# Cutting the first sequence into 256, 256 and 512 tokens and the last into 512, 384 and 128, in a software pipeline that took 512 tokens at a time

## What is computed

```python
x = L0_attn_x                                   # 4 x 1024 x 256
x = _layernorm(x + _L0_attn_ref(x, ...))        # conv, gates, recurrence h = a*h + b, out_w, RMS norm
x = _layernorm(x + relu(x @ W1 + b1) @ W2 + b2)
x = _layernorm(x + _L1_attn_ref(x, ...))        # in_proj, conv, x_proj, 16 states, out_proj
x = _layernorm(x + relu(x @ w1 + b1) @ w2 + b2)

def step(h, inp):                               # the state-space block, for each token t
    dA_t, dBx_t, C_t = inp
    h = dA_t * h + dBx_t                        # 256 channels x 16 states
    y_t = jnp.einsum('bdn,bn->bd', h, C_t)
    return (h, y_t)
```

## Time and profile before

| | us |
|---|---|
| median of 3 runs (1019.75 to 1020.57) | 1020.5 |
| the profiled execution, its own time | 1020.38 |
| its span, first to last instruction | 1018.6 |
| busy in the span: PE / DVE / ACT / POOL | 788.0 / 800.8 / 604.5 / 556.9 |

### The profile page before, as it was taken

The page is one execution under the profiler, slowest core; times in us unless marked ns, Lnnn a source line. Parts: engine busy times, 40 slices in busy tenths (PEclk is TensorE's granted clock), DMA queues, the critical chain, the costliest instruction groups (busy, mean ns, idle before and its releaser), DMA issues. The chain is left out here.

```text
span 1018.6 us, 8402 instructions
## 1 busy us (share of the span) xinstructions
PE 788.0 (77%) x2536; PEld 484.5 (48%) x2536; DVE 800.8 (79%) x970; ACT 604.5 (59%) x983; POOL 556.9 (55%) x419
## 2 busy tenths in 40 slices
PE   1439639855998999899979997999799796469275
PEld 0216225523553755475537553755375545226134
DVE  0400331999899999999999999999999999999711
ACT  3432745575758685868586858685857473443131
POOL 3041162257845785589457855894576466545510
PEclk9659878977999999999999999999999898589588
DMA  9000000000000010001000100010000000000000
GB/s 319 10 21 21 0 21 11 11 0 21 1 0 1 1 62 1 0 1 63 0 2 1 62 1 0 1 42 0 1 1 21 1 1 1 21 0 1 21 1 21
DMA packets 9213, 19.41 MB, mean 19 GB/s; under 512 B 1360, under 2 KB 3920, under 8 KB 9168
## 3 DMA queue, kind: packets, MB, share of 16 engines
q1 hardware_dynamic: 9168, 18.88, 5.4%
HBM read 14.68 MB, written 4.19 MB: 19 GB/s over the span
## 5 line engine op out<-in xcount | busy, mean ns | idle before, releaser
L350 POOL TENSOR_TENSOR y<-y,hC 128x1024 f32<-128x1024 f32 x112 | 271.9, 2428 | 120.0 <-DVE hC L915 116.9
L1102 PE MATMUL pC<-w,hT 128*128 128x256 f32 x1024 | 229.6, 379 | 2.3 <-ACT hT L546 2.3
L608 ACT ACTIVATE dA<-dt,A_neg 128x512 f32<-128x512 f32 x256 | 173.1, 715 | 89.2 <-DVE hs L904 88.9
L1102 PEld LDWEIGHTS pC<-w,hT 128*128 128x128 f32 x1024 | 194.0, 190 | 34.1 <-issue 4.7
L1223 PE MATMUL pS<-stack,sel 97*128 97x512 f32 x256 | 146.1, 604 | 73.7 <-DVE hs L904 73.6
L904 DVE TENSOR_TENSOR_SCAN hs<-dA,carry,pS 128x512 f32<-128x512 f32 x128 | 163.0, 1273 | 3.9 <-issue 0.4
L904 DVE TENSOR_TENSOR_SCAN hs<-dA,pS 128x512 f32<-128x512 f32 x128 | 155.3, 1214 | 9.0 <-DVE pS L889 5.4
L889 DVE TENSOR_TENSOR pS<-u,pS 128x1024 f32<-128x1024 f32 x128 | 154.9, 1210 | 2.1 <-PE pS L1223 1.8
L915 DVE TENSOR_TENSOR hC<-hs,pS 128x1024 f32<-128x1024 f32 x128 | 153.1, 1196 | 1.5 <-PE pS L1223 1.3
L1095 PE MATMUL pA<-tg,w 128*128 128x512 f32 x256 | 123.0, 623 | 16.4 <-ACT xi L554 14.5
L546 ACT ACTIVATE hT<-pA,ffb_sb 128x512 f32<-128x512 f32 x128 | 86.3, 682 | 82.6 <-PE pA L1095 82.6
(11 more groups left out here) (104 smaller groups left out, 1006.5 us busy)
## 6 DMA issues: line engine op xcount, KB each, us to landing
xt<-xT SPq DMA_DIRECT2D x8, 515.0 KB, 4.9
xtok<-x SPq DMA_DIRECT2D x8, 512.0 KB, 4.6
out<-x3b SPq DMA_DIRECT2D x8, 512.0 KB, 2.8
w<-w1a SPq DMA_DIRECT2D x1, 1024.0 KB, 9.1
w<-w2a SPq DMA_DIRECT2D x1, 1024.0 KB, 10.8
w<-w1b SPq DMA_DIRECT2D x1, 1024.0 KB, 8.3
w<-w2b SPq DMA_DIRECT2D x1, 1024.0 KB, 9.9
gate_w<-gateT SPq DMA_DIRECT2D x1, 512.0 KB, 7.0
```

Of the source, the lines that this page charges most:

```text
L350: nc.gpsimd.tensor_tensor(y[:, :, 0:ch.T], so_far, hC[:, n % CRING, :, 0:ch.T], ALU.add).then_inc(S["y_sum"], 1)
L608: nc.scalar.activation(dA[:, k % ARING, 0:ch.T], dt[:, h, 0:ch.T], ACT.Exp, scale=A_neg[:, h, n:n + 1]).then_inc(S["dA_ready"], 1)
L1102: mm = nc.tensor.matmul(dst[:, b * D:b * D + D], src(k, t0), w[:, k, :], start=k == 0, stop=k == nk - 1)
```

## The change

One line differs. It changes chunk lengths and with them the number of chunks, from 8 to 10, and of steps, from 12 to 14.

```diff
-SPLITS = ((512, 512), (512, 512), (512, 512), (512, 512))
+SPLITS = ((256, 256, 512), (512, 512), (512, 512), (512, 384, 128))
```

## The result

The changed kernel takes 1030.6 us (median of 4 runs, 1030.29 to 1030.95) where the kernel before, run beside it, takes 1020.5 (4 runs). The ratio is 1.0099, with a 95% interval of 1.0082 to 1.0117: 1% slower, 10.1 us. The prediction had slower as the likeliest side and 1024.3 us, 3.8 us more than before: the direction came, at well over twice the size.

The account below looks back on a forecast made before the run. VectorE was taken to bound full periods, one dependent chain the fill and drain. Front +4.4, middle -3.2 and -3.2, end +5.9 gave +3.9: span 1022.5, time 1024.3 us with 1.8 around it; range 1004 to 1038.

Parts of the forecast that it names:

- each step also holds the whole gate chain of a 512-token chunk, in order: Periods of chunks 0 and 1: the neighbour's chain sets their length, 78 and 90 us, against 57 and 65 DVE needs.
- Case A: Whole kernel: the ends gain, the short periods next to them hand it back; 1016 to 1032 us, centre 1024.3, chance 0.44.
- Rival B: Short periods of chunks 0 and 1 follow DVE and PE, near 66 and 76 us; centre 1011, chance 0.34.
- D: Whole kernel: fixed cost and gain cancel, DVE idle time falling by just 21 us; 1020.5 to 1025 us, chance 0.05.
- Rival C: Short states beside long PE blocks: DVE-PE round trip loses 0.4 us more in each of 32, +12, 1036 us; chance 0.17.
- If DVE waits on `pS` make more than 15 us in all, C is: Sign for the round-trip rival: DVE's waits for PE's spreads, summed, exceed 15 us.
- not on PE's spreads: Sign for the first two periods: DVE idle 20 to 25 us each, longest waits on ACT and POOL gate-chain pieces.
- 57 to `up`: Chunk 1's period: gate chain takes 57 us up to `up`, after a start of 12.5, within a 90 us period.
- 91.3: Chunk 7's period in us, with a prep chunk of 384 (-1.6) and a gate chunk of 128 (+4); before, 87.99.
- 17, 29 and four states of 1.6 to 2: Chunk 9's period: `up` at 17 us, 29 for `up`, `down`, spreads and waits, then four last states; put at 51.
- the first products of each burst run at 1.2 GHz: PE in the fill's step 0: granted clock 0.76; a burst after idle time loses about 2.7 us that half length doesn't halve.
- VectorE sets the pace: Full periods, such as chunk 2's: DVE busy 98.65 of 102.30 us is the bound; PE at 93.77 is close but not.

## Why the prediction was right

What it said would be seen, against the trace:

| | predicted | measured |
|---|---|---|
| first `u` | 109 | 110.3 |
| period of chunk 0 | 78 | 78.8 |
| of chunk 1 | 90 | 92.5 |
| of chunk 2 | 99 | 98.0 |
| of chunks 3 to 5 | 102 | 102.0, 102.0, 102.4 |
| of chunk 6 | 99 | 99.2 |
| of chunk 7 | 91.3 | 94.2 |
| of chunk 8 | 74.5 | 73.3 |
| of chunk 9 | 51 | 52.1 |
| drain | 24.5 | 23.8 |
| span | 1022.5 | 1028.5 |

The mechanism was right in its step "each step also holds the whole gate chain of a 512-token chunk, in order": the runs with the later norm, with quarters and with the cut in the middle show it for the front, and the one with halved products for the end. Case A came in, near its upper end. Rival B (the short periods follow DVE and PE) is out: they were 78.8 and 92.5, not 66 and 76. D had the work nearly right (DVE +25.0 busy, of which I had 21; 2.2 of the rest are the long `u` below), and the idle time wrong, as B had.

Rival C needs more care, because its sign came. "If DVE waits on `pS` make more than 15 us in all, C is": they make 26.3 + 9.3 = 35.6 us in the changed kernel, against 3.1 before. The rows for the whole span, after and then before:

```profile
DVE pS L889 <- PE pS L1223: 26.3, 15, 3.4
DVE hC L915 <- PE pS L1223: 9.3, 7, 2.7
```

```profile
DVE pS L889 <- PE pS L1223: 1.8, 2, 1.4
DVE hC L915 <- PE pS L1223: 1.3, 2, 0.9
```

8.4 us of them are in chunk 0's period, 11.1 in chunk 1's and 14.1 in chunk 9's, and so the sign "not on PE's spreads" for the first two periods didn't come either. What didn't come is C's price. It was 12 us on top of A, and the three periods that hold these waits are together 4.4 us above A's figures (223.4 against 219). So the sign was badly chosen: the spreads stand in PE's stream among the products of the long neighbour, and a chain that runs in order makes DVE wait for them too. A and C share this part. At the end it is the PE blocks ahead of the spreads (halving them moved the end by 5.7 us); in chunk 0's period 3 us on POOL, with no work on PE or DVE, moved it by 3.3, which C doesn't give.

The size was off by 6 us, in three terms (2.5, 2.9 and 1.3; the other marks take some 0.7 back):

- "57 to `up`" in chunk 1's period measured 60.2, and `up` up to the spread behind it 16.0 where I had 15.5, with its first eight products in 5.70 us; the start (12.2) and the rest (4.1) were 0.3 and 0.9 shorter than I had them. Together +2.5.
- "91.3" for chunk 7 measured 94.2. 2.2 us of this are its opening `u`, which lasted 3.42 us instead of 1.22:

```profile
785.13 5.65 POOL L350 TENSOR_TENSOR y<-y,hC 128x1024 f32<-128x1024 f32 x2
785.16 3.42 DVE L877 SCALAR_TENSOR_TENSOR u<-dt,v 128x1024 f32<-128x1024 f32 x1
```

A POOL sum began 0.03 us ahead of it; the two sums took 5.65 us, where two in a row take 4.86 elsewhere in this trace. The long `u` recurred with 3.42 us in the runs with the later norm and with halved products, was 1.37 in the one with doubled outputs and 1.55 in the run with only the last cut. In that last one POOL's sums began 0.43 us behind `u` and took 5.86 us. So it hangs on how the two meet; what they share there was not tried.
- The first `u` came 1.3 us later than 109, all of it in step 1 (47.3 us where I had 46); which link of its chain was longer I can't say.

Two sums of the prediction don't come out as they are written, and their slips cancel. The parts of chunk 9's period (17, 29 and four states of 1.6 to 2) give 52.4 to 54 and not 51; it measured 52.1. What is taken off the drain (20.5, 4.3, 9 and 2) leaves 22.7 and not 24.5; it measured 23.8. And "the first products of each burst run at 1.2 GHz" holds in step 0 for the output product and `up`, with a granted clock of 0.50 in the first 2.3 and 3.7 us, but not for the gate products, which stand at 1.00 although 16 of them took 9.37 us, against 7.03 in step 1.

The reading of the prediction that the runs refute didn't enter the sum: "VectorE sets the pace" in a full period. It does (18.2 us more of busy DVE time in chunk 4's period made it 17.7 longer), but the chain through POOL sets the same pace: 3.95 us more there made chunk 3's period 4.4 longer, so it had no slack to speak of.

## What to carry to other kernels

In this software pipeline, written in one fixed order, a step was at least as long as the longest role in it, so shortening one chunk gained only where its neighbours in the pipeline were short too. Look at each step's roles before you cut: at the front 256, 384, 384 won 7 us where 256, 256, 512, with the same number of chunks, lost 6. It is no rule for both ends, since 384, 384, 256 at the end lost 7. And a tightly ordered loop may sit on two bounds at once: an engine that is 97% busy is no proof that a delay elsewhere is free. Last, choose a sign that only one of the rivals gives: a wait that both give decides nothing.

## What the hardware showed that I had not expected

The state of PE's clock moved times by about 2 us a place in both directions: eight products of 512 columns took 3.60 to 3.70 us at a granted clock of 1.00, and 5.29 to 5.70 at 0.64 to 0.68. A delay of 3 to 4 us in the chain gave 2 back in this way. And the clock isn't fixed by the program: with the same 12 us of rows ahead, the gate products took 3.60 us in one execution and 5.29 in another. A DVE product over 1024 elements took 3.42 us instead of 1.22 where a POOL sum had begun 0.03 us ahead of it, and one over 512 took 2.88 instead of 0.69 (in the run cut in the middle) where one had begun 0.02 us ahead.
